# Attention stage of a decoder layer: reordered cross-layer product and activation copies, no ones column, and the division on GpSimd

## The reference

```python
x = x + attn(layernorm(x))           # linear attention, 16 heads of 8, causal running sums
x = x + xattn(layernorm(x), ctx)     # correlation of queries and keys picks 5 lags; values are mixed by them
x = x + ffn(layernorm(x))            # mixture of 8 experts, 2 per row

# attn, step by step over the 64 positions t of a sequence (b, h: sequence, head)
S = S + outer(k_t, v_t)              # 8 x 8 numbers for each head
z = z + k_t                          # 8 numbers for each head
out_t = (q_t @ S) / (q_t @ z + 1e-6)
```

## Time and profile before

| what | value |
|---|---|
| median of three runs | 744.52 us (739.71 to 746.67) |
| the profiled execution's own time | 746.59 us |
| its span (first to last instruction) | 744.6 us |
| mean granted PE clock over the span | 0.927 of full |
| busy: PE, DVE, POOL, ACT | 621.7, 538.9, 455.1, 390.9 us |
| attention stage | from 0 to about 315 us of the span |

### The profile page before, as it was taken

One profiled execution on the slowest core, in us unless ns is written; L12 is line 12 of the kernel. 1 busy time (PEld: TensorE's weight loads), 2 busy tenths in 40 slices (PEclk: granted clock), 3 DMA queues, 4 the chain that ended last, 5 costly groups with the idle time before them and its releaser, 6 DMA issues. The chain is left out here.

```text
span 744.6 us, 14383 instructions
## 1 busy us (share of the span) xinstructions
PE 621.7 (83%) x3260; PEld 418.8 (56%) x3261; DVE 538.9 (72%) x1797; ACT 390.9 (52%) x989; POOL 455.1 (61%) x518
## 2 busy tenths in 40 slices
PE   3989989999999997714877745599999999999995
PEld 1545555555555554313866635466666666666663
DVE  4699998899999988262798979656656666665652
ACT  3546666665666654302766620055566666666663
POOL 5899988888888882102444415665256666666662
PEclk9999999999999999555799956899999999999998
DMA  5400110000511013427445320021011111111110
GB/s 150 158 2 17 41 30 29 28 28 28 84 28 29 28 29 73 55 46 225 109 116 131 82 61 0 19 51 45 16 42 45 40 43 44 43 40 43 40 45 22
DMA packets 50610, 40.69 MB, mean 55 GB/s; under 512 B 21827, under 2 KB 40899, under 8 KB 50566
## 3 DMA queue, kind: packets, MB, share of 16 engines
q1 hardware_dynamic: 45574, 29.62, 15.7%
q0 software_dynamic: 4992, 10.56, 5.4%
HBM read 27.28 MB, written 12.88 MB: 54 GB/s over the span
## 5 line engine op out<-in xcount | busy, mean ns | idle before, releaser
L1065 PE MATMUL bank<-w_s,shared 128*128 (+1 forms) x312 | 148.7, 599 | 0.4
L462 POOL TENSOR_TENSOR shared<-v,qk 128x1152 f32<-128x1152 f32 x64 | 140.9, 2202 | 12.4 <-POOL qk L457 5.2
L1065 PE MATMUL bank<-shared,tri_s 128*128 128x360 f32 (+1 forms) x384 | 136.7, 493 | 2.2 <-DVE R L724 2.2
L523 POOL DMA_INDIRECT shared<-xs_d,row_u x92 | 88.6, 963 | 40.9 <-issue 24.6
L724 DVE TENSOR_TENSOR R<-bank,qk 128x360 f32<-128x360 f32 (+1 forms) x192 | 97.0, 549 | 20.2 <-PE bank L1065 17.6
L1033 DVE SCALAR_TENSOR_TENSOR hid<-bank,gt,shared 128x256 f32<-128x256 f32 x156 | 75.3, 483 | 49.6 <-ACT shared L668 48.3
L530 POOL DMA_INDIRECT out_x<-shared x64 | 63.1, 986 | 73.3 <-DVE shared L1057 58.3
L668 ACT ACTIVATE shared<-bank 128x256 f32<-128x256 f32 x156 | 59.9, 384 | 78.7 <-PE bank L1065 78.7
L1065 PEld LDWEIGHTS bank<-shared,tri_s 128*128 128x128 f32 x384 | 70.2, 192 | 45.6 <-issue 26.2
L730 DVE TENSOR_REDUCE nd<-R 128x144 f32<-128x1152 f32 x64 | 86.6, 1353 | 2.6
L1065 PE MATMUL bank<-w_s,ct 128*128 (+1 forms) x624 | 82.6, 275 | 0.2 <-issue 0.2
(11 more groups left out here) (211 smaller groups left out, 1148.9 us busy)
## 6 DMA issues: line engine op xcount, KB each, us to landing
xs_d<-xs SPq DMA_DIRECT2D x16, 270.0 KB, 3.5
X<-in_x SPq DMA_DIRECT2D x16, 256.0 KB, 2.8
ct<-in_ctx_t SPq DMA_DIRECT2D x16, 256.0 KB, 2.9
gram_d<-gd SPq DMA_DIRECT2D x16, 256.0 KB, 2.4
ct<-in_ctx_r SPq DMA_DIRECT2D x16, 256.0 KB, 3.8
circ<-prob_d SPq DMA_DIRECT2D x32, 64.0 KB, 2.6
w_s<-in_w_up SPq DMA_DIRECT2D x1, 2048.0 KB, 8.6
shared<-xs_d,row_u POOLq DMA_INDIRECT x92, 2.6
```

Source lines behind the costliest of these rows:

```text
L462: nc.gpsimd.tensor_tensor(outer[k], v9[k % 2][:].unsqueeze(3).broadcast_to([P, H, D1, D]), kk.unsqueeze(2).broadcast_to([P, H, D1, D]), AL ...
L523: nc.gpsimd.indirect_dma_start(xg[q], None, xs_d[:, :], bass.IndirectOffsetOnAxis(ap=rows, axis=0)).then_inc(xg_in[q], 16)
L1065: return nc.tensor.matmul(o, l, r, start=start, stop=stop, skip_group_check=True)
```

## The change

Four edits, all inside the slot functions of the attention stage.

1. The ones column goes. The value tile `vv` is 16 x 8, the product of k and v 1024 numbers. Two running sums of 512 columns take it (banks 2 and 3, `HALVES`), and a third of 128 columns sums k itself (bank 4), straight from `qk`. DVE multiplies twice 512 numbers and once 128, the last into column D of `R`. Two fills of the value tiles at the start of the kernel go with it.
2. The multiplication of numerators by reciprocals (into `on`) moves from DVE, where it stood right behind the reciprocals, to POOL (`divide`), where it stands behind `outer_product` of a1 tile 0 and `rstd` of a0. PE's transposes of `on` still wait for c_on.
3. On PE `project` of tile 0 moves ahead of the cross layer's key product; that product stands between the projections of tiles 0 and 1.
4. On ACT `a_evac_proj` of tile 0 moves ahead of the four `norm` activations of d.

```diff
--- before.py
+++ after.py
@@ -35,7 +35,7 @@
 NSORT = 8
 LN_EPS, ATT_EPS, RMS_EPS = 1e-5, 1e-6, 1e-6
 DIAG_PARTS = [(0, 8), (8, 14), (14, 16)]
-HEADS = [(0, 6), (6, 11), (11, 16)]
+HALVES = [(0, 8), (8, 16)]
 
 
 def need(eng, sem, count):
@@ -106,12 +106,12 @@
         xh = sb("xh", [P, GT, E])
         xT = sb("xT", [P, GW])
         ex, rl = [sb(f"ex{i}", [P, 2 * E]) for i in range(2)], [sb(f"rl{i}", [P, 2 * E]) for i in range(2)]
-        v9 = [sb(f"v9_{i}", [P, H, D1]) for i in range(2)]
+        vv = [sb(f"vv{i}", [P, H, D]) for i in range(2)]
         qk = [sb(f"qk{i}", [P, GT, 2 * E]) for i in range(2)]
 
         shared = sb("shared", [P, GT * H * D1 * D])
         bias_f, bias_r, bias_a, bias_b = (shared[0:3, i * NBIAS:(i + 1) * NBIAS] for i in range(4))
-        outer = [shared[:, i * H * D1 * D:(i + 1) * H * D1 * D].rearrange("p (h e d) -> p h e d", h=H, e=D1)
+        outer = [shared[:, i * H * D * D:(i + 1) * H * D * D].rearrange("p (h e d) -> p h e d", h=H, e=D)
                  for i in range(GT)]
         R = sb("R", [P, H, D1, D])
         nd = [sb(f"nd{i}", [P, GT, H, D1]) for i in range(2)]
@@ -422,15 +422,13 @@
             pool.memset(vo3[:], 0.0).then_inc(padded, 1)
             pool.memset(ones3[:], 1.0).then_inc(setup, 1)
             pool.memset(power[:], -0.5).then_inc(setup, 1)
-            for k in range(2):
-                pool.memset(v9[k][:], 1.0).then_inc(setup, 1)
             pool.memset(ones_f[:], 1.0).then_inc(setup, 1)
             pool.memset(picked[:], 0.0).then_inc(made, 1)
             pool.memset(e_pad[:], 0.0).then_inc(made, 1)
             pool.memset(zero[:], 0.0).then_inc(made, 1)
             pool.memset(power2[:], -0.5).then_inc(made, 1)
             pool.memset(used[0][:], 0.0).then_inc(s_used, 1)
-            pool.wait_ge(setup, 5)
+            pool.wait_ge(setup, 3)
 
             def rstd(g, p, stats, seen, ve, ve_sem, rs, rs_sem, mr, mr_sem, nb, nb_sem, normed):
 
@@ -460,8 +458,16 @@
                 need(pool, b_run, 3 * (t - GT) + 3)
                 kk = qk[p][:, k, E:2 * E].rearrange("p (h d) -> p h d", h=H)
                 nc.gpsimd.tensor_tensor(
-                    outer[k], v9[k % 2][:].unsqueeze(3).broadcast_to([P, H, D1, D]),
-                    kk.unsqueeze(2).broadcast_to([P, H, D1, D]), ALU.mult).then_inc(a_outer, 1)
+                    outer[k], vv[k % 2][:].unsqueeze(3).broadcast_to([P, H, D, D]),
+                    kk.unsqueeze(2).broadcast_to([P, H, D, D]), ALU.mult).then_inc(a_outer, 1)
+
+            def divide(g, p, r):
+
+                pool.wait_ge(c_den, 2 * g + 2)
+                need(pool, c_tr, g)
+                nc.gpsimd.tensor_tensor(
+                    on[:].rearrange("p t (h d) -> p (t h) d", h=H), nd[p][:, :, :, 0:D].rearrange("p t h d -> p (t h) d"),
+                    rden[:].unsqueeze(2).broadcast_to([P, GT * H, D]), ALU.mult).then_inc(c_on, 1)
 
             def slot(n, i):
                 a0, a1, c = stage(n, i, 2), stage(n, i, 1), stage(n, i, -1)
@@ -469,6 +475,8 @@
                     outer_product(*a1, 0)
                 if a0:
                     rstd(a0[0], a0[1], mv_a, a_mv, ve_a, a_ve, rs_a, a_rs, mr_a, a_mr, nb_a, a_nb, a_xh)
+                if c:
+                    divide(*c)
                 if a1:
                     outer_product(*a1, 1)
                     outer_product(*a1, 2)
@@ -561,7 +569,7 @@
                 nc.scalar.activation(ex[k % 2][:], bank[1][:, 0:2 * E], ACT.Relu, scale=-1.0).then_inc(a_pev, 1)
                 nc.scalar.activation(rl[k % 2][:], bank[1][:, 0:2 * E], ACT.Relu).then_inc(a_pev, 1)
                 need(act, a_outer, t - 1)
-                nc.scalar.activation(v9[k % 2][:, :, 0:D], bank[1][:, 2 * E:3 * E].rearrange("p (h d) -> p h d", h=H),
+                nc.scalar.activation(vv[k % 2][:], bank[1][:, 2 * E:3 * E].rearrange("p (h d) -> p h d", h=H),
                                      ACT.Copy).then_inc(a_pev, 1)
                 act.wait_ge(a_pev, 3 * t + 1)
                 nc.scalar.activation(ex[k % 2][:], ex[k % 2][:], ACT.Exp, scale=-1.0).then_inc(a_ex, 1)
@@ -576,12 +584,12 @@
                 a0, a1, c, d = (stage(n, i, s) for s in (2, 1, -1, -2))
                 if a1:
                     a_evac_xT(*a1)
+                if a1:
+                    a_evac_proj(*a1, 0)
                 if d:
                     g, p, r = d
                     need(act, d_tr, g)
                     norm(g, p, rs_c, nb_c, c_nb, xh2, d_xh)
-                if a1:
-                    a_evac_proj(*a1, 0)
                 if c:
                     act.wait_ge(c_tr, c[0] + 1)
                     need(act, c_y, c[0])
@@ -717,13 +725,14 @@
             def times_q(g, p, r, k):
                 t = GT * g + k
                 need(dve, b_red, t)
-                for c, (lo, hi) in enumerate(HEADS):
-                    n_h = hi - lo
+                qq = qk[p][:, k, 0:E].rearrange("p (h d) -> p h d", h=H)
+                for c, (lo, hi) in enumerate(HALVES):
                     dve.wait_ge(b_run, 3 * t + c + 1)
-                    qq = qk[p][:, k, lo * D:hi * D].rearrange("p (h d) -> p h d", h=n_h)
                     nc.vector.tensor_tensor(
-                        R[:, lo:hi], bank[2 + c][:, 0:n_h * D1 * D].rearrange("p (h e d) -> p h e d", h=n_h, e=D1),
-                        qq.unsqueeze(2).broadcast_to([P, n_h, D1, D]), ALU.mult).then_inc(b_mul, 1)
+                        R[:, lo:hi, 0:D], bank[2 + c][:].rearrange("p (h e d) -> p h e d", h=hi - lo, e=D),
+                        qq[:, lo:hi].unsqueeze(2).broadcast_to([P, hi - lo, D, D]), ALU.mult).then_inc(b_mul, 1)
+                dve.wait_ge(b_run, 3 * t + 3)
+                nc.vector.tensor_tensor(R[:, :, D], bank[4][:, 0:E].rearrange("p (h d) -> p h d", h=H), qq, ALU.mult).then_inc(b_mul, 1)
                 dve.wait_ge(b_mul, 3 * t + 3)
                 if k == 0:
                     need(dve, c_on, g - 1)
@@ -741,11 +750,6 @@
                                             ).then_inc(c_den, 1)
                     dve.wait_ge(c_den, 2 * g + 1)
                     nc.vector.reciprocal(rden[:], den[:]).then_inc(c_den, 1)
-                    dve.wait_ge(c_den, 2 * g + 2)
-                    need(dve, c_tr, g)
-                    nc.vector.tensor_tensor(
-                        on[:].rearrange("p t (h d) -> p (t h) d", h=H), nd[p][:, :, :, 0:D].rearrange("p t h d -> p (t h) d"),
-                        rden[:].unsqueeze(2).broadcast_to([P, GT * H, D]), ALU.mult).then_inc(c_on, 1)
                 if b:
                     times_q(*b, 1)
                 if a0:
@@ -1072,10 +1076,11 @@
             def running_sums(g, p, r, k):
                 t = GT * g + k
                 pe.wait_ge(a_outer, t + 1)
-                for c, (lo, hi) in enumerate(HEADS):
+                for c, (lo, hi) in enumerate(HALVES):
                     need(pe, b_mul, 3 * (t - 1) + c + 1)
-                    mm(bank[2 + c][:, 0:(hi - lo) * D1 * D], tri_s[:], outer[k][:, lo:hi].rearrange("p h e d -> p (h e d)")
-                       ).then_inc(b_run, 1)
+                    mm(bank[2 + c][:], tri_s[:], outer[k][:, lo:hi].rearrange("p h e d -> p (h e d)")).then_inc(b_run, 1)
+                need(pe, b_mul, 3 * t)
+                mm(bank[4][:, 0:E], tri_s[:], qk[p][:, k, E:2 * E]).then_inc(b_run, 1)
 
             def project(g, p, r, k):
                 t = GT * g + k
@@ -1093,16 +1098,17 @@
                     transposes(bank[0], xh).then_inc(a_tr, 1)
                 if b:
                     running_sums(*b, 1)
+                if a1:
+                    if i is None and a1[0] == 0:
+                        pe.wait_ge(setup, 3)
+                        pe.wait_ge(bias_ch, 8)
+                    project(*a1, 0)
                 if d:
                     g, p, r = d
                     pe.wait_ge(ct_in[p], 16 * r + 16)
                     need(pe, d_qT, g)
                     mm(bank[7][:], wk2_s[:], ct[p][:]).then_inc(d_k, 1)
                 if a1:
-                    if i is None and a1[0] == 0:
-                        pe.wait_ge(setup, 5)
-                        pe.wait_ge(bias_ch, 8)
-                    project(*a1, 0)
                     project(*a1, 1)
                 if c:
                     pe.wait_ge(c_on, c[0] + 1)
@@ -1208,7 +1214,7 @@
                         last = mm(bank[4][:, k * NE:(k + 1) * NE], xrT[:, k * P:(k + 1) * P], wr_s[:])
                     last.then_inc(f_sc, 1)
 
-            pe.wait_ge(setup, 9)
+            pe.wait_ge(setup, 7)
             cross_slots(cross_slot)
 
             pe.wait_ge(r_ch, START_READY)
```

## The result

The changed kernel took 836.5 us (median of four runs, 833.97 to 838.41) against 745.16: a ratio of 1.123 (95% interval 1.119 to 1.128). It is 91 us slower; 852 had been forecast, 812 to 872 as the range. Its profiled execution took 837.38 us, its span 835.1.

A forecast was written before the change was run, and what follows sets the result against it. POOL, running back to back, was taken to bound the 17.0 us slot. Circle 22.4, clock 2.6 and loop's turn 0.2 gave 25.2 us a slot; in total +107.6 on 746.6 made 854, 852 for the median, range 812 to 872.

The forecast's parts named there:

- the circle PE - ACT - POOL - PE: Attention slots 1 to 14: moved division closes a loop of waits, 22.4 us at full clock against 17.0; chance 0.75 with falling clock.
- Ones column: Dropping it shortens POOL's product by 0.20 us a tile, 0.81 us a slot; nothing gained or lost on DVE.
- Division: Numerators times reciprocals on POOL: 1.17 us plus 0.1 hand-over; DVE loses 0.69 us a slot.
- The 1.00 us wait: PE's wait ahead of `project` tile 1 in each slot, for tile 0's copies to empty bank 1; forecast to go.
- Start of the slot to the transposes: PE's transposes of `on` forecast 11.4 us into the slot, after idling 6 us from 5.4.
- The clock: PE falls to 1.2 GHz in each wait, about 5.2 us of work then at half rate, costing 2.6 us a slot.
- The loop's turn: 0.2 us added per slot: the difference between the mean slot of 17.2 us and the slot read.
- Slots 1 to 14: Attention slots held by the circle: together 348.1 us against 240.9, so +107.
- Slot 15: Division there waits for POOL's last product: `on` 0.9 us later than before.
- Slot 16 and the end: In slot 16 the longer division lies open, +0.5 us.
- the clock stays up: Rival, chance 0.14: PE keeps full rate in the waits, so 2.6 us fall away 14 times, 816 us.
- Not waited for: Rival, chance 0.04: division ends within 6 us of slot start, PE never waits; 731 us, or 745 if POOL bounds.

The follow-up runs named there:

- the first experiment: The changed kernel with the division put back on DVE, right behind the reciprocals, all else as changed; 754.2 us, ratio 1.014 to the kernel before.

## Why the prediction was right, and by how much not

The mechanism is shown. First the circle PE - ACT - POOL - PE: moving the division two pieces forward on POOL takes all of the loss away, one piece forward 27 us of it, and the division alone on the kernel before brings it, and more. Then the fall of the clock in each wait: filling the wait gives 23.4 us back. Step by step:

- **Ones column.** Product 1.95 us for 1.98. DVE's three pieces now come to 2 x 678 + 281 = 1637 ns, forecast 1649. "Nothing" for DVE was right in the changed kernel. For the edit alone it would have been wrong, through the collision; here `on` was no longer on DVE.
- **Division.** 1.07 for 1.17 us; the rows' own slope was near. The Trainium skill's ratio (GPSIMD Engine Reference, 3.1), measured there at 2048 numbers, would have given an estimate of 1.35; here, at 512, the ratio was 1.07 / 0.69 = 1.55.
- **The 1.00 us wait** went, and on the circle it was worth nothing, as said.
- **Start of the slot to the transposes.** 193.00 - 181.91 = 11.1 us, forecast 11.4: the division's 0.1, and the 0.42 for hand-over and weight load was too much, since the transposes began 0.06 us behind the division's end (191.87 + 1.07 = 192.94).
- **The clock.** This term was mis-sized. Transposes to the next slot: 205.81 - 193.00 = 12.8 us, against 10.97 at full clock: the fall costs 1.8 us, I took 2.6. PE was at half rate for 3.66 us after it resumed, against 5.8 us in the one earlier case that I took as the model. The forecast's 5.2 us leaned on that one case; its lower bound of 3.5 was close. The granted clock of the stage is 0.86, forecast about 0.8. With the wait filled the same stretch takes 11.05 us, so the 1.8 is the clock's.
- **The loop's turn.** I added 0.2 us a slot; the steady slots, 23.9 each, show none on the circle.
- **Slots 1 to 14.** +92.8 for +107: 14 x (0.8 + 0.3 + 0.2) = 18 less, of which slots 1 to 4 give 4 back (slot 2 took 26.1 us, the ring was still settling). Slot 15 +0.8 for +0.9. Slot 16 and the end: -2.8 - 0.8 = -3.6 for +0.5. The prediction had nothing for the clock there. In the kernel before it was at half from the wait at 295.18 to PE's last matmuls of the stage at 313. In the changed kernel it stayed at 1.00 behind the wait of 2.09 us at 375.19, and behind the one of 2.25 us at 386.90 it was low only from about 388 to 391 (0.50), then 0.99 to 400. Why it came back there and not before was not tried. The moment of the means therefore holds some 3 us that don't belong to the circle.

The errors nearly all point one way, so that 852 is within 2% of the result owes little to errors that cancel. In one statement the prediction was wrong without harm: that POOL's own work of 17.0 us in a slot was the bound of the kernel before, whatever the order. Part of it was time lost in the collision, and the reordering alone frees it. Of the rivals, "the clock stays up" (816) was out by the first trace. "Not waited for" had the right point of decision: with the division first in POOL's slot it ends about 6 us after a slot's start, and the loss is nothing (742.9).

## What to carry to other kernels

Before work is moved to another engine, ask what stands ahead of it in that engine's order, and whether any of that waits, by whatever way round, for the engine that will wait for the work. If so, the sum of the pieces around the ring is the new slot, however free the engines are; move the work to a place ahead of the piece that closes the ring. And price such a wait on PE twice, once for its length and once for the clock behind it.

## What was not expected

- **Products on DVE and POOL in each other's way.** DVE's product with both inputs in SBUF took 0.69 us alone or beside `rstd` and up to 2.07 beside POOL's product of 1024; POOL's add took 1.13 instead of 0.73 beside it. The rows look like one waiting for the other, not like both going slower: in the first experiment each held `on` ended 0.54 to 0.55 us behind POOL's product, and in the kernel before the add ended 0.59 us behind `on` (161.29 and 160.70). DVE's denominators, with one input in SBUF, were held as well, 0.71 for 0.21 us. DVE's products with one input in PSUM ran beside POOL's at their usual length (655 to 693 ns). The Trainium skill (GPSIMD Engine Reference, 8) names contention with DVE instructions in what it calls a 2-port perf mode or with two SBUF inputs: for `on` the traces agree, and whether the denominators ran in such a mode no run here shows. So the shares of two engines can each rest on an accident of timing: taking 11% off POOL's product cost some 6 to 13 us.
- **Chips differ.** The kernel before took 743.7 us on the chip of one series and 767.9 and 767.2 on the chips of the two others. The changed kernel's means came at 416.4 us in the first comparison, where the kernel before took 745.2, and at 417.0 on one of the slower chips, so the attention stage is the same; the rest of the span took 418.7 and 442.5 us. Why the later stages are slower there was not tried. Only ratios within a series, and the moment of the means, compare across them.
